# First projections and stacks of two attention stages made inside the stages ahead of them

## What is computed

```python
# layer 1 feed-forward: 16 experts of width 64 and a shared one, two experts of each token
gates = top2(sigmoid(x @ gate_w + gate_b))
x = layernorm(2 * x + shared(x) + sum_e gates[e] * expert_e(x))
# layer 2 attention: causal, 16 heads of width 8, x itself serves as the values
q, k = split(x @ W_attn + b_attn)
p_h  = softmax(causal(q_h @ k_h.T / sqrt(8)))
x = layernorm(x + sum_h (p_h @ x) * head_weights[h])
# layer 2 "ffn", first part: rotary attention, 16 heads of width 8
q, k, v = x @ Wq + bq, x @ Wk + bk, x @ Wv + bv
q, k = q * cos + rotate_half(q) * sin, k * cos + rotate_half(k) * sin
x1 = layernorm(x + softmax(q_h @ k_h.T / sqrt(8)) @ v @ Wo + bo) * g1 + be1
```

## Times and profile before

| | us |
|---|---|
| median of three runs | 6392.3 |
| lowest, highest | 6390.1, 6402.6 |
| profiled execution | 6393.6 |
| span in its trace | 6391.8 |
| stage `expert_ffn` | about 1445 to 1790 |
| stage `causal_attention` | 1790 to 2811 |
| stage `rotary_attention` | 2811 to about 3700 |

### The profile page before, as it was taken

The page is one execution under the profiler, slowest core; times in us unless marked ns, Lnnn a source line. Parts: engine busy times, 40 slices in busy tenths (PEclk is TensorE's granted clock), DMA queues, the critical chain, the costliest instruction groups (busy, mean ns, idle before and its releaser), DMA issues. The chain is left out here.

```text
span 6391.8 us, 88406 instructions
## 1 busy us (share of the span) xinstructions
PE 5689.2 (89%) x33302; PEld 2898.8 (45%) x33302; DVE 3942.1 (62%) x6471; ACT 2809.9 (44%) x4462; POOL 1043.2 (16%) x703
## 2 busy tenths in 40 slices
PE   4999996788959999958999988879999989997999
PEld 1333333444437777742222256653333433334666
DVE  5767774773357777738889722237767777674412
ACT  2656664321113333326777733324444444443333
POOL 0000000220002222211111000003333333242000
PEclk8999997788969999988999989989999999998999
DMA  3211110000021111012111100000000000001000
GB/s 75 44 31 32 32 19 11 0 0 12 0 48 34 28 27 29 16 37 38 31 29 33 16 28 1 1 18 11 11 11 15 11 11 14 8 15 37 4 4 7
DMA packets 119846, 132.59 MB, mean 21 GB/s; under 512 B 44730, under 2 KB 68074, under 8 KB 119098
## 3 DMA queue, kind: packets, MB, share of 16 engines
q1 hardware_dynamic: 119420, 126.95, 9.7%
HBM read 103.47 MB, written 22.07 MB: 20 GB/s over the span
## 5 line engine op out<-in xcount | busy, mean ns | idle before, releaser
L521 DVE TENSOR_REDUCE l_max_parts<-l_p 128x2 f32<-128x1024 f32 x512 | 602.8, 1220 | 219.8 <-PE l_p L497 179.8
L3064 DVE TENSOR_REDUCE wide_max_parts<-wide_p 128x2 f32<-128x1024 f32 x512 | 614.3, 1220 | 161.9 <-PE wide_p L2968 149.4
L667 ACT ACTIVATE attn_w<-l_p 128x512 f32<-128x512 f32 x1024 | 554.1, 596 | 363.8 <-PE l_p L657 275.5
L667 ACT ACTIVATE attn_w<-rot_p 128x512 f32<-128x512 f32 x1024 | 550.5, 597 | 263.1 <-PE rot_p L649 260.8
L521 DVE TENSOR_REDUCE rot_max_parts<-rot_p 128x2 f32<-128x1024 f32 x512 | 601.6, 1218 | 87.4 <-PE rot_p L497 85.2
L2079 PE MATMUL caus_p<-caus_x_one,big 128*128 128x129 f32 x4608 | 640.0, 286 | 13.0 <-ACT big L2139 13.0
L2139 ACT ACTIVATE big<-caus_p 128x512 f32<-128x512 f32 (+3 forms) x768 | 344.9, 489 | 632.8 <-PE caus_p L2065 483.1
L2079 PEld LDWEIGHTS caus_p<-caus_x_one,big 128*128 128x128 f32 x4608 | 590.0, 198 | 50.3 <-ACT big L2139 14.3
L2474 ACT ACTIVATE moe_hidden<-moe_experts,moe_b 128x512 f32<-128x512 f32 x512 | 351.5, 687 | 514.2 <-PE moe_experts L2462 514.2
L2987 PE MATMUL wide_p<-wide_q,wide_k 64*128 64x512 f32 x2048 | 530.7, 597 | 0.0
L3162 ACT ACTIVATE attn_w<-wide_p 128x1024 f32<-128x1024 f32 x342 | 349.6, 1024 | 362.0 <-PE wide_p L2987 360.8
(11 more groups left out here) (513 smaller groups left out, 8240.1 us busy)
## 6 DMA issues: line engine op xcount, KB each, us to landing
wide_inverse<-inverse_rows SPq DMA_DIRECT2D x64, 256.0 KB, 3.9
l_q_stack<-q_parts SPq DMA_DIRECT2D x288, 32.0 KB
l_k_stack<-k_parts SPq DMA_DIRECT2D x288, 32.0 KB
caus_q_stack<-q_parts SPq DMA_DIRECT2D x288, 32.0 KB
caus_k_stack<-k_parts SPq DMA_DIRECT2D x288, 32.0 KB
rot_q_stack<-q_parts SPq DMA_DIRECT2D x288, 32.0 KB
rot_k_stack<-k_parts SPq DMA_DIRECT2D x288, 32.0 KB
big<-in_L_ffn_W SPq DMA_DIRECT2D x32, 256.0 KB, 6.0
```

The source lines that it names most:

```text
L521: self.nc.vector.tensor_reduce(self.max_parts[:, 2 * p:2 * p + 2, n, half], pair[:, :, 0:self.width(n, half)], AX.X, ALU.max).then_inc(*se ...
L667: self.nc.scalar.activation(self.exps[t % len(self.exps)], bank, ACT.Exp).then_inc(*self.exped.up())
L3064: nc.vector.tensor_reduce(max_parts[:, :, n, h], side, AX.X, ALU.max).then_inc(*maxed.up())
```

## The change

The stacks and the arrays value, rest and parts move into a class `PairBuffers`, allocated once for three stages (`layer0` allocates its own). A `CausalStart` and a `RotaryStart` hold the weights, semaphores and projections of the two attention stages and are made ahead of `expert_ffn`.

- In `expert_ffn`, SP also issues the loads of the causal projections and the 27 fixed pieces. During batch 1, one step of the causal stage's batch 0 follows each expert pair: four `project` (PE, DVE), six `split` (all on POOL), then the stores and the fills of units 0, 1 and 2. To make room, the expert weights, gates and hidden buffers move into `attn_w` and `big`.
- In `causal_attention`, the plan begins with the maxima. SP issues the load of `head_w` and the 12 loads of the rotary stage. In the last batch, the 14 steps of the rotary stage's batch 0 (four `project`, four `rotate`, six `split`) go into the maxima of units 13 and 14, so they run during units 12 and 13. At the start of units 14 and 15 SP fills rotary units 0 and 1 into the slots just freed.
- In `rotary_attention`, the plan begins with the two `values` steps of batch 0 and goes on with the maxima. The fixed pieces are not loaded again.

```diff
+class PairBuffers:
+    SLOTS = 3
+    def __init__(self, st):
+        self.q_stack = [st.sbuf(f"q_stack{i}", [STACK, GROUP, T], BF16) for i in range(self.SLOTS)]
+        self.k_stack = [st.sbuf(f"k_stack{i}", [STACK, GROUP, T], BF16) for i in range(self.SLOTS)]
...
 def expert_ffn
+    early = ahead_of(after.begin_plan())
...
                 if m:
                     plan.append(("down", t, m - 1))
+                if b and m:
+                    plan += early[:1]
+                    early = early[1:]
...
             top.begin_on_sp()
+            after.begin_on_sp()
+            new = Fresh()
+            for (kind, *args), i, left in plan:
+                if kind == "next_split":
+                    after.proj.split_on_sp(sp, *args)
+                elif kind == "next_fill":
+                    after.fill_on_sp(sp, new, *args)
...
+                elif kind == "next_project":
+                    if new(after.loaded, after.LOADS):
+                        v.wait_ge(*after.loaded.at(after.LOADS))
+                    after.proj.project_on_dve(v, *args, bank)
...
+class CausalStart:
+    def begin_plan(self):
+        return self.proj.plan(0) + [("fill", u) for u in range(PairBuffers.SLOTS)]
...
 def causal_attention
-        steps[0] = ([("fill", 0)] if u == 0 else []) + steps[0]
...
-        if u + 1 < len(units):
+        if g in (1, 2) and b + 1 == nb:
+            for i, step in enumerate(ahead_of(after.begin_plan())[7 * (g - 1):7 * g]):
+                steps[2 + 3 * i] = [step] + steps[2 + 3 * i]
+        if u + 1 < len(units) and u + 1 >= heads.SLOTS:
             steps[8] = [("fill", u + 1)] + steps[8]
...
-    plan = [("begin", 0)] + proj.plan(0) + [step for more in m_steps[:26] for step in more]
+    plan = [("begin", 0)] + [step for more in m_steps[:26] for step in more]
...
+        if u + 2 >= len(units):
+            plan.append(("next_fill", u + 2 - len(units)))
...
-            heads.begin_on_sp()
+            after.begin_on_sp()
...
+                elif kind == "next_fill":
+                    u = args[0]
+                    n = heads.per_unit * (len(units) - heads.SLOTS + u + 1)
+                    if new(heads.scored, n):
+                        sp.wait_ge(*heads.scored.at(n))
+                    after.fill_on_sp(sp, new, u)
...
-            pe.wait_ge(*loaded.at(48))
...
+                elif kind == "next_rotate":
+                    after.proj.turn_on(pool, nc.gpsimd, *args)
+                elif kind == "next_split":
+                    after.proj.split_on(pool, nc.gpsimd, *args)
...
 def rotary_attention
-    plan = proj.plan(0) + weighted.plan([step for u in range(len(units)) for step in maxima(u)], 8,
+    plan = [("values", 0, 0), ("values", 0, 1)] + weighted.plan([step for u in range(len(units)) for step in maxima(u)], 8,
                                         finish)
...
-            pe.wait_ge(*w_loaded.at(16 * W_LOADS))
```

More of the change, by code:

```diff
@@ L1758, with ahead_of, expert_ffn @@
 E1, I1 = 16, 64
-def expert_ffn(core):
+def ahead_of(steps):
+    return [("next_" + kind, *args) for kind, *args in steps]
+def expert_ffn(core, after):
     st = Stage(core, "moe1")
@@ L1939, in _, with __init__, begin_on_sp, fill_on_sp @@
                     turn.on_act(a, c, xc[:, c * BANK:(c + 1) * BANK], bank)
-    st.close()
-def causal_attention(core):
+        @block.gpsimd
+        def _(pool):
+            for (kind, *args), i, left in plan:
+                if kind == "next_split":
+                    after.proj.split_on(pool, nc.gpsimd, *args)
+    st.close()
+class CausalStart:
+    LOADS = 32
+    def __init__(self, core, buffers):
+        self.st = st = Stage(core, "caus0")
+        self.inp, self.nc, nb = core.inp, core.nc, core.n_batch
+        self.w, self.bias = st.sbuf("w", [P, 2 * C]), st.sbuf("bias", [P, 2])
+        self.loaded = st.sem("loaded")
+        self.units = [(b, g) for b in range(nb) for g in range(H // GROUP)]
+        self.heads = PairHeads(st, buffers, len(self.units), GROUP * (BANK // P + NT), causal=True)
+        self.proj = Projections(st, buffers, {"q": self.w[:, 0:C], "k": self.w[:, C:2 * C]},
+                                {"q": self.bias[:, 0:1], "k": self.bias[:, 1:2]})
+    def begin_plan(self):
+        return self.proj.plan(0) + [("fill", u) for u in range(PairBuffers.SLOTS)]
+    def begin_on_sp(self):
+        for dst, src in ((self.w, self.inp["L2_attn_W_attn"]), (self.bias, self.inp["L2_attn_b_attn_c"])):
+            self.nc.sync.dma_start(dst[:, :], src[:, :]).then_inc(*self.loaded.up(16))
+        self.heads.begin_on_sp()
+    def fill_on_sp(self, sp, new, u):
+        b, g = self.units[u]
+        self.proj.stored_on_sp(sp, new, b)
+        self.heads.fill_on_sp(sp, new, u, b, g)
+def causal_attention(core, begun, after):
     st = Stage(core, "caus")
@@ L2015, in causal_attention @@
         "turn": lambda c: (turn.kept, c + 1),
+        "next_project": after.proj.released()["project"],
+        "next_rotate": after.proj.released()["rotate"],
         **proj.released()}))
@@ L2086, in _ @@
                     turn.on_pe(x[:, 4 * c:4 * c + 4, :], bank)
+                elif kind == "next_project":
+                    if new(after.loaded, after.LOADS):
+                        pe.wait_ge(*after.loaded.at(after.LOADS))
+                    if new(turn.kept, HALF):
+                        pe.wait_ge(*turn.kept.at(HALF))
+                    after.proj.project_on_pe(*args, bank)
+                elif kind == "next_rotate":
+                    after.proj.rotate_on_pe(pe, *args, bank)
         @block.vector
@@ L2096, in _ @@
                     proj.project_on_dve(v, *args, bank)
-                elif kind == "split":
-                    if args[1] == 0:
-                        proj.split_on(v, nc.vector, *args)
+                elif kind == "next_project":
+                    n = args[0]
+                    if new(after.loaded, after.LOADS):
+                        v.wait_ge(*after.loaded.at(after.LOADS))
+                    if new(proj.stored[n], 16 * nb):
+                        v.wait_ge(*proj.stored[n].at(16 * nb))
+                    after.proj.project_on_dve(v, *args, bank)
+                elif kind == "next_rotate":
+                    after.proj.rotate_on_dve(v, *args, bank)
                 elif kind == "max":
@@ L2188, in rotary_attention @@
+def rotary_attention(core, begun):
     st = Stage(core, "rot")
@@ L3418, in build @@
         st.close()
-        for stage in (position_bias, layer0, ternary_ffn, linear_attention, expert_ffn,
-                      causal_attention):
+        for stage in (position_bias, layer0, ternary_ffn, linear_attention):
             stage(core)
         with nc.sbuf_tensor("x_mid", [P, n_batch * NT, C], F32) as core.x_mid:
-            rotary_attention(core)
+            st = Stage(core, "pair")
+            buffers = PairBuffers(st)
+            rotary = RotaryStart(core, buffers, n_batch * H // GROUP)
+            causal = CausalStart(core, buffers)
+            expert_ffn(core, causal)
+            causal_attention(core, causal, rotary)
+            causal.st.close()
+            rotary_attention(core, rotary)
+            rotary.st.close()
+            st.close()
             block_experts(core)
```

172 lines of the change are left out of this document (95 added, 77 removed).

## The result

The changed kernel has a median of 6297.35 us (6293.80 to 6304.87, four runs). The kernel before, run beside it, has 6393.61 us (6390.11 to 6402.61). The ratio is 0.9849 with a 95% interval of 0.9832 to 0.9866, so the change makes the kernel faster by 1.5%, some 96 us. The forecast was 6299.

A forecast was written before the change was run, and what follows sets the result against it. PE's work sets the time in most stages, except the waiting causal and rotary starts and DVE-bound leads. Starts -113.6, expert stage +3.4, last causal batch +16, unit 14 +1 give -93.2 us: 6299, range 6283 to 6315.

The forecast's parts named there:

- Causal start, -51.0: Start of causal stage: first maxima matmul comes some 0.4 us after the barrier instead of 51.4, gaining 51.0 us.
- Rotary start, -62.6: Start of rotary stage: DVE's first maximum comes some 5 us after the barrier instead of 67.6, gaining 62.6 us.
- The leads stay: Maxima-only stretches of about 30 us behind both starts: bound by DVE, kept whole at 30 and 29 us, clock 0.50.
- The rival that the clock comes back earlier: First exponentials of both stages: full clock returns sooner, 5.5 us less in each, 6288; chance 0.07.
- Expert stage, +3.4: Expert stage: four added projections cost PE's time, 0.86 us each, 3.4 us in all, bounds 0 and 7.
- Last causal batch, +16: Causal units 12 and 13: eight added PE steps cost 2.0 us each, 16 us, bounds 6.9 and 24.
- they cost only PE's time: Rival for the last causal batch: its eight steps cost PE's own time, 6.9 us, total 6290; chance 0.10.
- POOL: Rival in causal units 12 and 13: POOL's added work holds DVE up, 25 us more, 6324; chance 0.03.
- Unit 14, +1: Causal unit 14: the second half's send waits behind the rotary fill, a tie costing 1 us, bounds 0 and 6.
- The sum: Whole kernel: -113.6 + 3.4 + 16 + 1 = -93.2 us, giving 6299; chance 0.54 as it stands.
- Slower than before: Rival: POOL falls behind in units 12 and 13, delaying fill and unit 14's send, to pass 6393.6; chance 0.02.
- the gap stays: Rival: first maxima wait for something unseen, 80 us return as a stall ahead of the lead, 6380; chance 0.02.

The follow-up runs named there:

- first experiment: Against the changed kernel, the rotary stage makes its first projections, splits and fills itself again; fixed pieces still not reloaded: 6346.88 us, ratio 0.9926.
- after: The changed kernel itself, against the kernel before: median 6297.35 us, ratio 0.9849; its profiled execution took 6293.8 us.

## Why the prediction was right, step by step

- **Causal start, -51.0.** Right: 51.2. It was sized from the order of time, border to border, and not from busy time. The loads and `head_w` were feared to take 25 us; SP's issue of the first unit's sends ended at 1810.82, 12.1 us ahead of PE's first exact scores at 1822.94, and the lead didn't grow. The margin was larger than the 5 us forecast because the 25 us were sized with a mean rate of 105 GB/s, taken over a stretch in which the queue also stood idle; the view of DMA by slices has the 2.7 MB of this start through within some 14 us.
- **Rotary start, -62.6.** Right: 63.2, of which 58.2 belong to the early work and 5.0, mostly a shorter wait for loads, to the fixed pieces (first experiment).
- **The leads stay.** Right: 29.7 and 29.2 us, DVE busy over 90%, clock 0.50 and, in the rotary one, 0.54. The rival that the clock comes back earlier fell: over the 20 us from the first exponential the granted clock is 0.73 before and after in the causal stage, and 0.86 and 0.81 in the rotary one.
- **Expert stage, +3.4.** Right: 3.5, and batches 2 and 3 as they were. PE's own time was the price, POOL, SP and DVE were beside it.
- **Last causal batch, +16.** Wrong in size. Units 12 and 13 grew by 8.7, and this falls outside the 10 to 20 us that the forecast itself named as its test. The term that was mis-sized is the price of a step, 2.0 us. The earlier trace rows compare pairs with a different granted clock, 0.92 and 0.94, and 3.1 of the 8.8 us between them go with that. Against a kernel without the rotary steps, at the same time at half clock, the eight cost 8.4 us, 1.05 each, between PE's 0.86 and the 1.3 of the rotary pairs, which the forecast had worked out and then set aside because another stage's ring of banks differs. That leaves 1.05 against the 1.4 of the causal pairs at equal clock, and no run explains this rest. The rival "they cost only PE's time", 6.9, was nearer than the value taken.
- **POOL.** Rival refuted: the work taken away changed nothing.
- **Unit 14, +1.** The mechanism is real and the tie as described, but it fell on the good side by 0.7 us. Unit 14 still grew, by 2.6, at a clock of 0.92 in place of 0.97. It grew by 2.1 at that clock in the kernel without any rotary step or fill too, and with the fill behind it but a clock of 0.97, in the kernel with PE kept busy, it took 58.5 us, as long as before. So that is the clock's doing and not the queue's.
- **The sum.** Forecast -93.2 for the span, measured -99.8. Of the 6.6 us between them units 12 to 14 are 5.7 (16 + 1 forecast, 11.3 measured), the two starts 0.8 and units 0 to 11, taken as unchanged, 1.2; the rest went 1.1 the other way. The medians differ by 96.3, so the forecast came out 1.7 us high. The total was right because the starts are 114 of it and their size was read off directly; the price of a step was twice the measured one. That the median came within 1.7 us is partly luck: the trace lies 6.6 us under the sum, but it is of the fastest of four runs, and their median is 3.5 us higher.
- **Slower than before**, and **the gap stays**: neither showed. POOL was never late for the fill, which SP began 2.1 us ahead of unit 14's first exponential, and nothing stood ahead of the first maxima.

Left open: why the time at half clock falls in the units where it falls. It isn't scatter from run to run: units 12 to 14 take 188.2 us with the same three clocks in after and in the kernel with the causal lead early. But it changes with edits that leave the units alone (unit 14 has 0.97 before, 0.92 in the kernel with the causal half alone), and no run separates the cause. Nor is it known why the clock of the filled lead stayed low; matmuls over all 128 rows in the lead were not tried.

## What to carry to other kernels

Measure a stall at a stage's start border to border in order of time, and look for what is late next: here it was a lead on another engine, which could then be moved ahead in the same way for another 40 us. Price moved work by the same engine's rhythm in the receiving stage, and distrust a comparison of two stretches that differ in more than the work, be it the granted clock or the places of the steps. Where PE is near its bound, read the clock beside the time of each stretch, since part of a gain or a loss comes and goes with it.

## What was not expected of the hardware

- **In a PE-bound stretch the clock moves with an edit, and hides part of it.** Units 12 to 14 hold 23.7 us at half clock with the eight matmuls, 18.2 with sixteen and 30.3 with eight quarter-size ones, although PE is busy over 90% of the three units in each. Of 6.9 us of PE's work added 5.2 came through, and of 5.2 taken away 0.3. It follows no order by work: 17.9 us with the same eight after an edit of the leads, and 17.6 and 24.0 with none of them.
- **A busy PE can stay at half clock throughout.** 18.75 of 21 us at work on 32-row matmuls, clock 0.50 to the end of the lead.
- **Work on POOL beside DVE was free** with DVE busy 93 of 127 us: 21 us taken away, 0.0 gained.
